# Attention with routed experts on one core: the first stacks' rows copied inside SBUF, the second batch's timetable a period later, and period 0 reordered

## The chip, the cores and the metric

The kernel runs on one core of one Trainium2 chip, and every time is a device time in microseconds (us). The core has a matrix engine, TensorE (PE, with PEld for its weight loads), VectorE (DVE), ScalarE (ACT), GpSimd (POOL) and SyncE (SP). Each runs its own instruction list in order and waits on semaphores. DMA transfers are issued here from the lists of SP and ACT, for the indirect ones from POOL.

## The reference

Input `x` has 16 batches of 512 tokens with 256 features, all float32. Two branches read a layer-normalised `x` and both are added to `x`:

```
xn = layernorm(x)
# attention, 16 heads of 16
q = rms_norm(xn @ Wq.T per head, qn_w);  k = rms_norm(xn @ Wk.T per head, kn_w);  v = xn @ Wv.T
attn = softmax(q @ k.T / 4);  A = (attn @ v) @ Wo.T
# routed experts: 8192 tokens, 8 experts, 1024 tokens each
scores = layernorm(xn) @ centroids.T
for each expert in turn: take the 1024 best tokens that are still free
F = routed + gelu(layernorm(routed) @ w1 + b1) @ w2 + b2, put back in token order
out = x + A + F
```

The products are kept close to float32 by splitting each operand into a rounded part (`hi`) and the rest (`lo`) and adding three products.

## The kernel before

**Stages.** A start-up brings in the weights and the first two batches. Then 16 batches of attention run, each in 8 periods, and in their gaps the engines prepare the next batches and route the tokens. The experts follow. The change is in the start-up and in the periods of the first batch (period 0 to 7, `at` in the code).

**One period.** `heads` (L482) makes a 128-key block of the scores of two heads; there are 32 calls per batch (`HS`) and 4 per period. Each result is turned into exponentials by ScalarE (`softmax`, L706), which needs it before PSUM's two buffers `S` come free. `weigh` (L498) multiplies them by `v`. In the same period TensorE does one item of preparation: a projection for q or k (`project_qk`, L439) or for v (`project_v`, L457), and in the first 28 periods a transposition of the normalised `x` of a later batch (`turn_x`, L415, with `score_x`, L426, for the routing scores every other period).

**From q and k to the stacks.** A projection goes from PSUM to `raw` by a DVE transposition (`turn_raw`, L839). It is squared, the squares are summed (`sum_squares`, L846), ScalarE makes the inverse root (`inverse_rms`, L685), POOL multiplies (`scale_qk`, L1216), DVE turns it back into `full` (`turn_back`, L853), and POOL splits it into `hi` and `lo` (`split_qk`, L1233). `heads` reads `stack`, in which rows 4e to 4e+3 of a tile hold hi or lo rows of one feature e for a pair of heads. Rows of 32 partitions have to be spread over every fourth partition, so `put_part` (L306) writes hi and lo to a DRAM buffer `parts`, and `stack_rows` (L321) reads them back, 6 transfers per half batch `u`. Row 3 is a constant: 0 in q's stack, 1 in k's, set by two memsets of DVE (L1047) and two of POOL (L1268).

**The first half batch.** It has its own functions, which share the squares and the scaling between ACT and POOL: `first_square`, `first_inverse_rms`, `first_round` on ACT, `first_sums`, `first_rest` on DVE and `first_scale_qk` on POOL. `first_stack` (L341) puts k's parts from SP's list (q's are put from ACT's list), and then reads the rows of the first two pairs of heads by 6 transfers (semaphore `c_stack`, 96), and of the last two by 6 more. The heads begin when `c_stack` has 96.

**The timetable.** Which period prepares what is given by `qk_at`, `v_at`, `squares_at` and `back_at` (L108 to L128), and by `scored` (L95) for the `x` of later batches. Before, the second batch (nb = 1) has its first two q and k projections ahead of period 0, together with `score_x(1)`; the other two are in periods 0 and 1, v in periods 2 and 3.

**Data for later batches.** `moments` (L768) reads an `x` tile on DVE, POOL makes the inverse deviation (`first_power`, L1185), `norm_x` (L786) normalises the tile in place in four DVE instructions, `turn_x` transposes it by TensorE. `split_x` (L1199) on POOL makes `xh` and `xl` of a batch, from which the projections read.

Of the kernel before, what the change touches and what calls it, by code (L numbers as in the profile page):

```python
# [135 lines left out]
def attention_and_routing(nc, a, out, k, ctx):  # L136
# [203 lines left out]

    def first_stack(e):  # L341

        now, then = slice(0, 2), slice(2, 4)
# [4 lines left out]
        stack_rows(e, 0, "k", 0, 0, now, c_stack)  # L350
        stack_rows(e, 0, "k", 0, 2, now, c_stack)
        e.wait_ge(s_part["k", "lo"], 16)
        stack_rows(e, 0, "k", 1, 1, now, c_stack)
        e.wait_ge(c_dve, 1)
        e.wait_ge(s_part["q", "hi"], 16)
        stack_rows(e, 0, "q", 0, 0, now, c_stack)
        stack_rows(e, 0, "q", 0, 1, now, c_stack)
        e.wait_ge(s_part["q", "lo"], 16)
        stack_rows(e, 0, "q", 1, 2, now, c_stack)
# [1483 lines left out]
```

## Time and profile before

| | us |
|---|---|
| median of 3 runs | 1056.38 (1056.06 to 1056.43) |
| the profiled execution's own time | 1055.93 |
| its span (first to last instruction) | 1054.2 |
| TensorE busy | 1023.1 (97% of the span), 6703 matmuls |
| DVE / ACT / POOL busy | 841.9 / 745.0 / 713.3 |
| start of the first `heads` call | 35.20 |

The profile counts an engine as busy while an instruction of it runs. Waits stand as idle time ahead of an instruction, with the engine that ended the wait. The granted TensorE clock is given as a share of full speed: 1.00 is 2.4 GHz and 0.50 is 1.2 GHz.

### The profile page before, as it was taken

Reading aid. Unit: us, or ns where it says so; the run is one execution under the profiler, and the core shown is the slowest. Engines: PE = TensorE matmul, PEld = TensorE weight load, DVE = VectorE, ACT = ScalarE, POOL = GpSimd, SP = SyncE. Lnnn points to the kernel's source line nnn. Section 1 sums busy time; section 2 is a strip of 40 time slices with the busy share of each in tenths; the row PEclk is TensorE's granted clock in tenths of the full one; section 3 lists DMA queues with packets and bytes.
Section 4 is the critical chain, followed back from the end, with each engine's and each line's share of the span. In section 5 each row is a group of like instructions: output and inputs, shape, how many; then the busy total and the mean of one; then the engine's idle time right before and its main releaser. Section 6 shows DMA issues by size and latency. Waiting matters only on the chain.

```text
span 1054.2 us, 19787 instructions
## 1 busy us (share of the span) xinstructions
PE 1023.1 (97%) x6703; PEld 643.0 (61%) x6703; DVE 841.9 (80%) x1922; ACT 745.0 (71%) x966; POOL 713.3 (68%) x753
## 2 busy tenths in 40 slices
PE   4899999999999999999999999999999999999997
PEld 3445555545454554454454443588888888888886
DVE  8999997787878788788778875797888788787872
ACT  3688888878888888888888889764655455465550
POOL 5677978776766767767767758666656666765434
PEclk9999999999999999999999999999999999999999
DMA  4544745344444443543533546143524344453313
GB/s 152 199 162 141 235 159 169 131 157 154 152 141 150 165 155 124 186 149 117 202 130 127 195 158 220 51 137 60 130 47 124 86 89 96 87 130 51 66 21 40
DMA packets 83527, 138.13 MB, mean 131 GB/s; under 512 B 9809, under 2 KB 35793, under 8 KB 83409
## 3 DMA queue, kind: packets, MB, share of 16 engines
q1 hardware_dynamic: 54560, 103.09, 28.7%
q0 software_dynamic: 12288, 16.79, 9.5%
q10 hardware_dynamic: 16560, 16.78, 4.9%
q8 instruction: 62, 1.02, 0.4%
q14 instruction: 57, 0.46, 0.1%
HBM read 86.28 MB, written 50.33 MB: 130 GB/s over the span
## 4 chain that ended last, share of the span: by engine, by line
PE 88%; DVE 6%; issue 2%; ACT 2%; POOL 1%; POOLq 0%; ACTq 0%; DVEq 0%
PE pv L509 19%; PE S L1476 17%; PE S L494 14%; PE W L1491 11%; PE W L453 9%; PE W L1493 6%; PE W L478 5%; PE W L464 4%; DVE xb L789 2%; ACT prob L710 1%; PE R L423 1%; PE R L1462 1%; PE pv L1462 1%; DVE raw L844 1%; PE R L434 0%
## 5 line engine op out<-in xcount | busy, mean ns | idle before, releaser
L710 ACT ACTIVATE prob<-S 128x1024 f32<-128x1024 f32 x512 | 496.1, 1023 | 91.0 <-PE S L494 90.1
L509 PE MATMUL pv<-prob,v 128*17 128x512 f32 x2048 | 246.5, 596 | 0.6 <-DVE oT L877 0.6
L494 PE MATMUL S<-stq,stk 64*128 64x512 f32 x1024 | 194.3, 452 | 5.5 <-ACT prob L710 4.1
L494 PEld LDWEIGHTS S<-stq,stk 64*128 64x128 f32 x1024 | 84.2, 184 | 130.5 <-ACT prob L710 111.7
L1758 POOL DMA_INDIRECT out<-prob,order_rows x64 | 103.4, 1615 | 58.7 <-DVE prob L1698 51.4
L509 PEld LDWEIGHTS pv<-prob,v 128*17 128x17 f32 x2048 | 46.2, 96 | 113.7 <-issue 112.3
L1554 ACT ACTIVATE wq_act<-S,b 128x512 f32<-128x512 f32 x64 | 44.0, 687 | 92.4 <-PE S L1476 92.1
L1214 POOL TENSOR_TENSOR sq<-raw 128x512 f32<-128x512 f32 x62 | 64.6, 1042 | 64.3 <-DVE raw L844 42.3
L1476 PE MATMUL S<-raw_nT,xT_w 128*128 128x512 f32 x384 | 91.2, 395 | 0.0
L1244 POOL TENSOR_TENSOR lo<-full,hi 128x512 fp32r<-128x512 f32 x62 | 80.4, 1297 | 5.0
L1476 PEld LDWEIGHTS S<-raw_nT,xT_w 128*128 128x128 f32 x384 | 71.6, 188 | 18.0 <-issue 1.7
L1476 PE MATMUL S<-hi,xT_w 128*128 128x512 f32 x256 | 81.5, 394 | 0.0
L877 DVE STREAM_TRANSPOSE oT<-pv 128x512 f32<-128x512 f32 x64 | 45.2, 707 | 31.6 <-PE pv L509 31.4
L1220 POOL TENSOR_TENSOR raw<-raw,rs 128x512 f32<-128x512 f32 x31 | 33.4, 1077 | 53.4 <-ACT rs L694 53.4
L944 DVE SCALAR_TENSOR_TENSOR ge<-R,cand 128x448 bf16<-128x448 f32 (+1 forms) x70 | 55.7, 796 | 2.6
L789 DVE TENSOR_SCALAR xb<-xb,mv,rstd 128x256 f32<-128x256 f32 x64 | 56.3, 938 | 0.8 <-POOL rstd L1190 0.8
L1554 ACT ACTIVATE wk_act<-S,b 128x512 f32<-128x512 f32 x64 | 43.9, 685 | 17.4 <-PE S L1476 16.4
L1476 PEld LDWEIGHTS S<-hi,xT_w 128*128 128x128 f32 x256 | 48.2, 188 | 11.2
L1773 POOL TENSOR_TENSOR e_va<-e_mv,eps_ln 128x4 f32<-128x4 f32 x16 | 8.3, 520 | 68.5 <-DVE e_mv L1612 68.5
L947 DVE TENSOR_REDUCE part_cnt<-ge 128x7 bf16<-128x448 bf16 (+1 forms) x70 | 51.0, 729 | 2.4
L844 DVE STREAM_TRANSPOSE raw<-W 128x512 f32<-128x512 f32 x64 | 45.0, 703 | 9.7 <-PE W L453 9.7
L453 PE MATMUL W<-xh,wq 128*128 128x512 f32 x128 | 49.8, 430 | 1.4 <-DVE xl L808 0.8
(258 smaller groups left out, 2464.1 us busy)
## 6 DMA issues: line engine op xcount, KB each, us to landing
stk<-parts SPq DMA_DIRECT2D x93, 256.0 KB, 3.8
stq<-parts SPq DMA_DIRECT2D x93, 256.0 KB, 4.3
xT<-in_w SPq DMA_DIRECT2D x32, 512.0 KB, 4.8
parts<-hi SPq DMA_DIRECT2D x63, 256.0 KB, 2.1
parts<-lo SPq DMA_DIRECT2D x63, 256.0 KB, 2.1
out<-ao ACTq DMA_DIRECT2D x32, 256.0 KB, 2.8
xb<-in_x ACTq DMA_DIRECT2D x13, 512.0 KB, 4.3
xb<-in_x SPq DMA_DIRECT2D x2, 512.0 KB, 5.7
```

Source lines behind the costliest of these rows:

```text
L453: ins = e.matmul(W[i % 2][:, :], w[n][pw][:, d, u * P:(u + 1) * P], (xh, xl)[px][nb % 2][:, d, :], start=(j == 0), stop=(j == 5))
L494: ins = e.matmul(S[n % 2][:, h, :], stack["k"][u][64 * h:64 * h + 64, p, c * P:(c + 1) * P], stack["q"][u][64 * h:64 * h + 64, p, :], star ...
L509: ins = e.matmul(pv[32 * j:32 * j + VW, :], v[b % 2][:, c, 8 * u + 4 * g + j, :], prob[(2 * t + j // 2) % RING][:, j % 2, :], start=(c == ...
L710: e.activation(prob[n % RING][:, :, :], S[n % 2][:, :, :], ACT.Exp).then_inc(s_exp, 1)
L789: ins = e.tensor_scalar(xb[m % XB][:, c, :], xb[m % XB][:, c, :], mv[m % 2][:, c, 0:1], rstd[m % 2][:, c:c + 1], ALU.subtract, ALU.mult)
L1214: e.tensor_tensor(sq[:, n, :], raw[u][:, n, :], raw[u][:, n, :], ALU.mult).then_inc(s_sq, 1)
L1244: e.tensor_tensor(lo[:, i, :], full[:, i, :], hi[:, i, :].bitcast(F32), ALU.subtract).then_inc(s_lo, 1)
L1476: ins = e.matmul(up[fc % UP], w1[pw][d][:, fc // 4, fc % 4 * P:(fc % 4 + 1) * P], nT[n % 2][px][:, d, :], start=(i == 0), stop=(i == 5))
L1491: e.matmul(down[c % 2][:, :], hid[n % 2][0][fc][:, tokens], both, start=(fc == 0), stop=(fc == NFC - 1), skip_group_check=True)
L1493: ins = e.matmul(down[c % 2][:, 0:D], hid[n % 2][1][fc][:, tokens], both[:, 0:D], start=False, stop=(fc == NFC - 1), skip_group_check=True)
L1554: e.activation(act[fc % UP], up[fc % UP], ACT.Gelu_apprx_tanh, bias=b1[:, n // U, fc:fc + 1]).then_inc(f_act, 1)
L1758: e.indirect_dma_start(out=out, out_offset=bass.IndirectOffsetOnAxis(ap=order[:, CH * n + c:CH * n + c + 1], axis=0), in_=y[u][:, c, :], i ...
```

## The change

- Rows of the first half batch's stacks, for the first two pairs of heads, are copied from `hi` and `lo` to the stack within SBUF by 12 transfers of 64 KB each (`first_rows`): 8 from SP's list (k's six, q's two of lo) and 4 from ACT's (q's rounded ones), ahead of q's `put_part`. `first_stack` keeps the way by DRAM for the last two pairs.
- q's second stack is set to zero by an ACT activation (`blank_stack`) and no longer by DVE. `tokens`, `cand` and `iota` are loaded behind `x` of batch 1 and `wo`, with a semaphore of their own (`c_table`).
- The squares of the second half of batch 0 are made by ACT (`later_square`), not POOL. DVE's order in the start-up changes: `norm_x(0)` ahead of `split_weights("q")`, `second_variance(0)` later, both `first_rest` ahead of `norm_x(1)`, and both variances and sums ahead of `split_first(1)`.
- Projections 0 and 1 of batch 1 and `score_x(1)` move from the start-up into period 0, projections 2 and 3 to periods 1 and 2, v to 3 and 4, the sums of squares to 2 and 5. With them DVE's `turn_raw(1, 0)`, both `turn_back(0, 1)`, `keep_score`, `turn_raw(1, 1)` and `moments(2)` come into period 0, and `split_weights("o")` into period 2. TensorE's wait for `wo` moves to `project_o`.
- POOL: `square(0, 3)`, `square(0, 2)` and `square(1, 0)` leave the start-up; `split_x(2)` comes in period 4, not 5.

```diff
@@ timetable
 def qk_at(nb, i):
+    if nb == 1:
+        return (0, 0, 1, 2)[i]
     return PERIODS * (nb - 2) + 6 + i if i < 2 else PERIODS * (nb - 1) + i - 2
 def v_at(nb, i):
+    if nb == 1:
+        return 3 + i
 def squares_at(nb, u):
+    if nb == 1:
+        return (2, 5)[u]
@@ attention_and_routing
-    CONSTS = 9
+    CONSTS = 6
+    TABLES = 3
+    FIRST_ROWS = 12
@@ get_stack
+        elif u:
+            e.wait_ge(c_blank, 1)
@@
+    def first_rows(e, n, part, r):
+
+        i = "qk".index(n)
+        for p in range(2):
+            e.dma_start(stack[n][0][r:P:4, p, :].bitcast(F32),
+                        (hi if part == "hi" else lo)[32 * p:32 * p + 32, i, :].bitcast(F32)).then_inc(c_stack, 16)
+
     def first_stack(e):
+        then = slice(2, 4)
+        e.wait_ge(c_pool, 1)
+        e.wait_ge(s_hi, 1)
+        first_rows(e, "k", "hi", 0)
+        first_rows(e, "k", "hi", 2)
+        e.wait_ge(s_lo, 1)
+        first_rows(e, "k", "lo", 1)
+        e.wait_ge(c_dve, 1)
+        e.wait_ge(s_lo, 2)
+        first_rows(e, "q", "lo", 2)
         put_part(e, 0, 0, "k", "hi")
         put_part(e, 0, 0, "k", "lo")
...
@@ sync_program
...
         load_x(e, 1)
         e.dma_start(land["o"], a["wo"]).then_inc(c_w["o"], 16)
+        for dst, src in ((tokens[:, :], a["tokens"]), (cand[:, :, :], a["cand"]), (iota[:, :], a["iota"])):
+            e.dma_start(dst, src).then_inc(c_table, 16)
         load_x(e, 2)
@@ project_o
+        if b == 0 and i == 0:
+            e.wait_ge(c_hi, 4)
+            e.wait_ge(c_lo, 4)
@@ heads
         if n == 0:
-            e.wait_ge(c_stack, 96)
+            e.wait_ge(c_stack, 16 * FIRST_ROWS)
+        elif n == 1:
+            e.wait_ge(s_xT, 4)
@@ tensor_program
         ins.then_inc(c_oc, 1)
-        project_qk(e, 1, 0)
-        project_qk(e, 1, 1)
-        score_x(e, 1)
-        e.wait_ge(c_hi, 4)
-        e.wait_ge(c_lo, 4)
...
                 if at:
                     weigh(e, 2 * at - 2)
+                else:
+                    project_qk(e, 1, 0)
...
-                        if m < B and qk_at(m, i) == at:
+                        if m < B and qk_at(m, i) == at and (at or i):
                             project_qk(e, m, i)
+                if at == 0:
+                    score_x(e, 1)
@@
+    def blank_stack(e):
+
+        e.wait_ge(c_zero, 1)
+        e.activation(stack["q"][1][:, :, :], zero[:, 0:1].unsqueeze(2).broadcast_to([P, 4, N]),
+                     ACT.Copy).then_inc(c_blank, 1)
+
+    def later_square(e, n):
+
+        e.wait_ge(s_raw, 4 - n)
+        e.wait_ge(c_ssq if n else s_ssq, 1)
+        e.activation(sq[:, n, :], raw[1][:, n, :], ACT.Square).then_inc(s_sq, 1)
@@ scalar_program
             e.activation(w[n][0][:, :, :], land[n], ACT.Copy).then_inc(c_hi, 1)
+        blank_stack(e)
         round_first(e, 0)
...
         first_round(e, 1)
+        later_square(e, 1)
+        later_square(e, 0)
         first_round(e, 0)
+        e.wait_ge(c_dve, 1)
+        e.wait_ge(s_hi, 2)
+        first_rows(e, "q", "hi", 0)
+        first_rows(e, "q", "hi", 1)
         put_part(e, 0, 0, "q", "hi")
         put_part(e, 0, 0, "q", "lo")
         round_first(e, 1)
+        inverse_rms(e, 0, 1)
         keep_first(e, 1)
-        inverse_rms(e, 0, 1)
@@ vector_program
-        for u in range(2):
-            ins = e.memset(stack["q"][u][:, :, :].bitcast(F32), 0.0)
-        ins.then_inc(c_dve, 1)
+        e.memset(stack["q"][0][:, :, :].bitcast(F32), 0.0).then_inc(c_dve, 1)
...
         moments(e, 0)
         split_weights(e, "k")
+        norm_x(e, 0)
         split_weights(e, "q")
-        norm_x(e, 0)
...
         first_sums(e, 1)
+        turn_raw(e, 0, 0)
         second_variance(e, 0)
-        turn_raw(e, 0, 0)
         first_sums(e, 0)
         turn_back(e, 0, 0, "k")
         turn_raw(e, 0, 3)
-        first_rest(e, 1)
         turn_raw(e, 0, 2)
         turn_back(e, 0, 0, "q")
+        first_rest(e, 1)
+        first_rest(e, 0)
         norm_x(e, 1)
-        first_rest(e, 0)
+        second_variance(e, 1)
+        sum_squares(e, 0, 1)
+        split_first(e, 1)
         copy_v(e, 0, 1)
         copy_v(e, 0, 0)
-        split_first(e, 1)
...
+                if at == 0:
+                    turn_raw(e, 1, 0)
+                    turn_back(e, 0, 1, "k")
+                    turn_back(e, 0, 1, "q")
+                    keep_score(e, 0)
+                    turn_raw(e, 1, 1)
+                    moments(e, 2)
+                    keep_score(e, 1)
...
+                if at == 2:
+                    split_weights(e, "o")
@@ split_qk (POOL)
+            if half == 1 and n == "k":
+                e.wait_ge(c_stack, 16 * FIRST_ROWS)
@@ gpsimd_program
         second_power(e, 0)
-        square(e, 0, 3)
-        square(e, 0, 2)
         second_power(e, 1)
         scale_qk(e, 0, 1)
         first_power(e, 2)
-        square(e, 1, 0)
         split_qk(e, 0, 1)
...
-                if nb < B and (back_at(nb, 0) + 1 == at):
+                if nb < B and back_at(nb, 0) + (nb > 1) == at:
                     split_qk(e, nb, 0)
...
-                if b + 2 < B and kk == (3 if b == 3 else 5):
+                if b + 2 < B and kk == {0: 4, 3: 3}.get(b, 5):
                     split_x(e, b + 2)
```

## Rows read from the trace of the kernel before

**Rows 1.** Windows: stretch, length, busy us (and instructions) per engine, clock, DMA share, GB/s.
```profile
150.00:750.00 600.00, 596.36 (x4172) 319.44 (x4173) 472.85 (x1082) 489.67 (x590) 426.26 (x454) 1.00 0.45 148
```
**Rows 2.** Timeline of PE: start, us, line, instruction, count, idle before and releaser.
```profile
27.38 1.10 PE L423 MATMUL S<-ident,xb 128*128 128x128 f32 x8 [1.35 <-DVE xb L789]
...
28.98 0.61 PE L574 MATMUL pv<-cent,onf 128*128 128x8 f32 x4
...
35.20 0.73 PE L494 MATMUL S<-stq,stk 64*128 64x512 f32 x4 [1.16 <-issue]
...
45.91 0.60 PE L423 MATMUL R<-ident,xb 128*128 128x128 f32 x4
...
47.10 1.91 PE L509 MATMUL pv<-prob,v 128*17 128x512 f32 x16
...
57.26 0.73 PE L494 MATMUL S<-stq,stk 64*128 64x512 f32 x4
```
**Rows 3.** Waits of PE from 45 to 75 us: total, times, longest.
```profile
PE R L423 <- DVE sT L828: 1.0, 1, 1.0
PE S L494 <- ACT prob L710: 0.7, 2, 0.4
PE W L453 <- POOL xl L1207: 0.5, 1, 0.5
```
**Rows 4.** Timeline of DVE, start-up and period 0.
```profile
3.43 1.76 DVE L1047 MEMSET stq<- 128x2048 f32 x1 [0.38 <-issue]
...
6.18 1.34 DVE L775 BATCH_NORM_STATS2 st<-xb 128x6 f32<-128x256 f32 x4
...
9.68 1.38 DVE L789 TENSOR_SCALAR xb<-xb,mv,rstd 128x256 f32<-128x256 f32 x4 [0.34 <-POOL rstd L1190]
...
21.22 0.70 DVE L862 STREAM_TRANSPOSE full<-raw 128x512 f32<-128x512 f32 x1
...
24.76 2.57 DVE L789 TENSOR_SCALAR xb<-xb,mv,rstd 128x256 f32<-128x256 f32 x4
27.25 0.74 DVE L821 SCALAR_TENSOR_TENSOR lo<-full,wq_col,hi 128x512 fp32r<-128x512 f32 x1
...
30.84 0.32 DVE L828 STREAM_TRANSPOSE sT<-R 128x128 f32<-128x128 f32 x1
...
31.53 1.21 DVE L851 TENSOR_REDUCE ssq<-sq 128x64 f32<-128x1024 f32 x1
...
41.31 3.83 DVE L789 TENSOR_SCALAR xb<-xb,mv,rstd 128x256 f32<-128x256 f32 x4
```
**Rows 5.** DMA issues from 0 to 60 us: queue, count, KB each, median us to landing.
```profile
xb<-in_x ACTq DMA_DIRECT2D x1, 256.0 KB, 3.9
```
**Rows 6.** Timeline of POOL.
```profile
8.30 1.34 POOL L1190 TENSOR_TENSOR rstd<-veps,half 128x4 f32<-128x4 f32 x1 [1.99 <-DVE veps L784]
...
22.00 1.06 POOL L1231 TENSOR_TENSOR raw<-raw,rs 128x512 f32<-128x512 f32 x1 [1.41 <-ACT rs L677]
```
**Rows 7.** Timeline of ACT.
```profile
12.33 0.60 ACT L659 ACTIVATE xh<-S 128x512 fp32r<-128x512 f32 x1 [4.40 <-PE S L423]
...
24.86 0.72 ACT L683 ACTIVATE hi<-full,wq_col 128x512 fp32r<-128x512 f32 x1 [2.28 <-DVE full L862]
```
**Rows 8.** Tile parts, 0 to 70 us, its DMAs from issue to landing.
```profile
DMA to landing us min/median/max: 2.0/2.8/4.3
```
**Rows 9.** Timeline of SP's DMA issues: start, us that the issuing took, count.
```profile
28.53 2.11 SPq L324 DMA_DIRECT2D stq<-parts  x3
...
46.47 1.90 SPq L324 DMA_DIRECT2D stq<-parts  x3
```
**Rows 10.** Chain that ended last, merged: start, us, engine, line, count.
```profile
38.24 2.41 PE W L453 x6
...
71.08 1.66 PE W L453 x6
```
**Rows 11.** Windows, the stretch at the lower clock; columns as in rows 1.
```profile
38.30:42.20 3.90, 3.90 (x14) 1.98 (x18) 3.00 (x6) 2.01 (x3) 3.82 (x5) 0.56 0.34 126
```

More of the change, by code:

```diff
@@ L252, in attention_and_routing @@
     c_xh = [sem(f"c_xh{m}") for m in range(2)]
-    c_x0, c_ssq, c_lg, c_rs, c_col, c_stack = (sem(f"c_{n}") for n in ("x0", "ssq", "lg", "rs", "col", "stack"))
+    c_x0, c_ssq, c_lg, c_rs, c_col, c_stack, c_table, c_zero, c_blank = (
+        sem(f"c_{n}") for n in ("x0", "ssq", "lg", "rs", "col", "stack", "table", "zero", "blank"))
     s_x = [sem(f"s_x{i}") for i in range(XB)]
@@ L339, in get_stack @@
         stack_rows(e, u, "q", 1, 2)
-    def first_stack(e):
-        now, then = slice(0, 2), slice(2, 4)
+    def first_rows(e, n, part, r):
[3 more added lines that the diff above has]
+                        (hi if part == "hi" else lo)[32 * p:32 * p + 32, i, :].bitcast(F32)).then_inc(c_stack, 16)
+    def first_stack(e):
+        then = slice(2, 4)
[8 more added lines that the diff above has]
+        first_rows(e, "q", "lo", 2)
         put_part(e, 0, 0, "k", "hi")
         put_part(e, 0, 0, "k", "lo")
-        e.wait_ge(c_pool, 1)
         e.wait_ge(s_part["k", "hi"], 16)
[L350 to L359, printed above, removed]
         stack_rows(e, 0, "k", 0, 0, then)
         stack_rows(e, 0, "k", 0, 2, then)
+        e.wait_ge(s_part["k", "lo"], 16)
         stack_rows(e, 0, "k", 1, 1, then)
+        e.wait_ge(s_part["q", "hi"], 16)
         stack_rows(e, 0, "q", 0, 0, then)
         stack_rows(e, 0, "q", 0, 1, then)
+        e.wait_ge(s_part["q", "lo"], 16)
         stack_rows(e, 0, "q", 1, 2, then)
@@ L401, in sync_program @@
                 shift_sync(e, 2 * b, 0)
-            if b:
-                put_parts(e, b, 1)
+            put_parts(e, b, 1)
             get_stack(e, b, 1)
@@ L593, in tensor_program @@
                         e.wait_ge(s_stack[u], 96 * (b + 1))
-                        e.wait_ge(c_stack, 96)
+                        e.wait_ge(c_stack, 16 * FIRST_ROWS)
+                        e.wait_ge(s_xT, 4)
                         if b or u:
@@ L1045, in vector_program @@
     def vector_program(e, x):
-        for u in range(2):
-            ins = e.memset(stack["q"][u][:, :, :].bitcast(F32), 0.0)
-        ins.then_inc(c_dve, 1)
+        e.memset(stack["q"][0][:, :, :].bitcast(F32), 0.0).then_inc(c_dve, 1)
         e.memset(pv[:, :], 0.0).then_inc(c_pv, 1)
-        for t, val in ((eps_rms, RMS_EPS), (slot, 0.0), (csum, 0.0), (zero, 0.0), (ones_h, 1.0)):
+        for t, val in ((eps_rms, RMS_EPS), (slot, 0.0), (csum, 0.0), (ones_h, 1.0)):
             e.memset(t[:, :], val)
+        e.memset(zero[:, :], 0.0).then_inc(c_zero, 1)
         e.memset(centg[:, :, :], 0.0).then_inc(c_gain, 1)
@@ L1106, in vector_program @@
                         shift_vector(e, 2 * b + kk // 4)
+                if at == 0:
[6 more added lines that the diff above has]
+                    keep_score(e, 1)
                 ex, i = routed(at)
                 if at == ROUTE:
+                    e.wait_ge(c_table, 16 * TABLES)
                     e.memset(taken, 0.0)
@@ L1128, in vector_program @@
                     for i in range(4):
-                        if m < B and qk_at(m, i) + 1 == at:
+                        if m < B and qk_at(m, i) + 1 == at and (at > 1 or m == 1 and i > 1):
                             turn_raw(e, m, i)
@@ L1239, in split_qk @@
                 e.wait_ge(s_part[n, "hi"], 16 * half)
+            if half == 1 and n == "k":
+                e.wait_ge(c_stack, 16 * FIRST_ROWS)
             e.tensor_copy(hi[:, i, :], full[:, i, :]).then_inc(s_hi, 1)
```

13 lines of the change are left out of this document (1 added, 12 removed).

## Prediction

> **What bounds the kernel now.** I read the windows first. From 150 to 750 us TensorE is busy for 596.36 of 600 us [rows 1], so in the long stretch nothing but TensorE's own work counts, and the change neither adds nor removes a matmul. It can gain only where TensorE idles: before the first heads and in the first batch. The timeline of PE gives the first: the heads begin at 35.20, after 1.16 of "issue", which no semaphore explains: it is the register load of `needed` and its branch, since TensorE's last work ended at 34.04 [rows 2]. The third view is PE's waits from 45 to 75 us: 1.0, 0.7 and 0.5, together 2.2 us [rows 3]. The fourth is the timeline of DVE, which ran through the start-up and the first periods with hardly a gap and is what TensorE waited for at 27.38 (1.35) [rows 2, 4]. After the first batch hardly a wait is left, so what TensorE is ahead at the end of batch 0 it is ahead at the end. The sum is made in the profiled execution's own terms, 1055.93 us (span 1054.2, 1.7 around it); the median of the runs is 0.45 higher, and I add that at the end.
>
> **The start of DVE.** One memset of 1.76 and the gap of 0.38 ahead of it go to ACT, 2.14 in all. The statistics of the first tile, at 6.18, need the tile's second half, which was issued at about 0.8 and took 3.9 to land: 4.7 [rows 4, 5]. Its first half can be read before that, so they begin at about 4.45 and the gain is 1.7, not 2.14. POOL does not take it back: it had idled 1.99 when it began the power at 8.30, so it is free at 6.3, and in the new order it is wanted at 6.6 [rows 6]. `norm_x(0)` moves from 9.68 to 8.0. The moved memset is an ACT activation of 2048 columns, four times the 0.60 of 512 columns: 2.4 at most, less if part of the 0.60 is fixed. ACT idled 4.40 ahead of 12.33 and must be free at 10.6, so 2.4 are hidden; without that cover it would cost itself [rows 7]. The three table loads that go behind `x` of batch 1 and `wo` free the constants sooner; `c_table` is asked for 32 periods later. Both cost nothing.
>
> **From q and k to hi and lo.** k's `full` came at 21.22, behind the sums of q's squares. It gains the 1.7, and 0.3 more because `second_variance` no longer stands ahead of `turn_raw(0, 0)`: 19.3 [rows 4]. q's scaling by POOL ended at 23.06, now 21.1, and q's turn back follows at once, at 21.2, since `first_rest` of k is moved behind it [rows 6]. ACT has two squares of 0.6 to make before it rounds q: from 20.5 to 21.8, so q's rounding starts at 21.8 in place of 24.86 [rows 7]. DVE then makes k's rest and q's rest, 0.7 each, to 23.3; q's came at 27.25 before. `norm_x(1)` follows. It took 2.57 with POOL's squares beside it and `norm_x(0)` 1.38 with POOL idle; the squares are gone, so I take 1.4, with 2.57 as the other end: done at 24.7, not 27.33 [rows 4]. TensorE turns the tile at 24.8 and has 2.2 of work to the end of the offset product (27.38 to 29.59) [rows 2]: 27.0. The two projections and `score_x(1)` that followed are now in period 0, the 1.16 stays. The heads could start at 28.2, which is 7.0 earlier.
>
> **The row transfers.** q's rounded rows are issued from ACT behind the rounding, at 22.5, four of them. The three row issues at 28.53 took 2.11 [rows 9], 0.7 each, so the last is out at 25.3; a transfer from or to `parts` landed after 2.0 to 4.3, median 2.8 [rows 8]. A copy within SBUF has no row. I take 2.4 (between the shortest and the median, since these move less): 27.7, just hidden. From 2.0 to 4.3 the rows are there from 27.3 to 29.6, so a start at 29.7 is the late end. SP's eight are issued from 20.6 on and as early. Behind ACT's four stand q's two `put_part` and `round_first(1)`, wanted at 25.4; they are done issuing near 26.0, which could delay `split_first(1)` by a few tenths. The rows of the last two pairs go out near 28 to 32 and are wanted at 41. The Trainium skill speaks against this part: "DMA: Bandwidth & Descriptors", Rules for kernel authors, says that many small transfers should be made into one and that under 64 KB one pays mostly overhead. No run here shows that yet; if it ruled, twelve transfers in place of six would eat what leaving DRAM out gives.
>
> **Period 0 and 1.** Here most of the 7.0 is lost again. After `norm_x(1)` DVE has a variance (0.5), the sum of squares (1.21), and two splits and two copies of 0.65: 29.0 [rows 4]. Projection (1, 0) waits for the last copy and takes 1.5 [rows 10]: 30.5. Then DVE's list is in series: `turn_raw` 0.65, two turns back 1.3, `keep_score` 0.7 (30.84 to 31.53), `turn_raw` 0.65: 33.8. From the statistics to the normalising it was 3.5 with a power of 1.34, the later power is 1.0: 3.2, so `norm_x(2)` starts at 37.0. POOL's `split_qk(0, 1)`, which stands behind the same power, runs beside it as it did before, when it took 3.83: 40.9 [rows 4, 6]. `turn_x(2, 0)` goes at 41.0 in place of 45.91 [rows 2]: 4.9 earlier. TensorE is there at 38.1 (period 0 ends at 33.5; then heads 1.3, weighing 1.85, a projection 1.5) and idles 2.9. At 45.91 all four projections were done; now one (1.5) is still to come: 3.4 ahead in work. The first late thing is therefore DVE, not the stack.
>
> **The rest of batch 0.** The old waits of 2.2 go, because the fuller periods 2 to 4 no longer outrun ACT, and `split_x(2)` comes a period earlier; I added up each engine's list period by period with the durations above (a normalising of four instructions lasts as long as the four POOL instructions beside it). TensorE comes to `turn_x(4, 0)` in period 5 at 61.3, and DVE is done with `norm_x(4)` and `keep_score(3)`'s transposition at 61.9, so 0.6 is left there, and 0.4 for ACT: 1.2 more. 3.4 + 1.2 = 4.6. The second half's stack: its last row issues ended at 48.4 and landed by 52.7 before period 4 began at 57.26 [rows 2, 8, 9]; now 3.1 earlier, 49.6, and wanted at 52.5. It stays hidden, with 2.9 in hand. The wait of `split_qk(0, 1)` for `c_stack` is met since 28, the new wait for `c_blank` too.
>
> **The clock.** At 38.3 to 42.2 the granted clock was 0.56 in the mean: after a stretch with few matmuls it fell to 1.2 GHz and came back [rows 11]. There a projection took 2.41 in place of 1.66 [rows 10], but TensorE would have waited for `norm_x(2)` anyway, so before it was nearly free. Now the long idle stretch is the 2.9 ahead of 41.0, and what follows is TensorE's own work. If the clock falls there for as long (3.4 us at half speed, from 0.56 over 3.9), half of it is lost: 1.7 at most; part of it may fall on waits. I take 1.6: 4.6 - 1.6 = 3.0. So the forecast is 1055.93 - 3.0 + 0.45 = 1053.4.
>
> **Rivals.**
> A, the forecast, one low stretch behind the idle time: 1053.4, its own range 1052.5 to 1054.2. Chance 0.46.
> B, no low stretch in the first periods, or one that falls on waits: 4.6 earlier, 1051.8 (to 1051.0 if `norm_x(2)` meets less of POOL). For it: idle times of 1.35 and 1.16 did not lower the clock. Against it: the new one is twice as long. Chance 0.21.
> C, the row transfers end the wait: twelve issues and landings of 4.3, or ACT's list late, start the heads at 29.7 or later and shift all behind by 1.5, and the low stretch comes too: 1054.9. Chance 0.16. This is where the Trainium skill's rule on small transfers would act.
> D, the early start is hidden anyway, no change: DVE and POOL bind the first batch so tightly that the later timetable of batch 1 (scaling, splitting and `split_x(2)` in one period and a half of POOL) gives back what period 0 gained, as a wait of 2 to 3 for `norm_x(4)` or for the projections of batch 2: 1056.2. Chance 0.11.
> E, slower: TensorE's clock stays low after the idle time of period 1 because the waits for DVE at the odd periods keep it from coming back. Each us at 1.2 GHz costs 0.5, so from 9.2 us of it on the 4.6 are gone; with 13.6 (four stretches like that of rows 11) it costs 6.8: 1055.93 + 2.2 + 0.45 = 1058.6. Against it: the one stretch of before ended by itself. Chance 0.06.
>
> **How the numbers follow.** About 0.2% (2.1 us) is what a measurement of this kernel can tell from no change, so faster means below 1054.3. A gives 0.44 of its 0.46, B 0.21, C 0.06: 0.71. Slower, above 1058.5, is only the worse part of E: 0.04. The rest, 0.25, is the same. The range leaves out the best part of B and the worse half of D and E: 1051.5 to 1056.1.
>
> **What would show it.** First statistics at 4.4 to 4.7 and `norm_x(0)` near 8.0; no DVE row for the second stack's memset; first heads at 28 to 29.7 with about 1.2 of issue ahead (right) or with a DMA ahead (C); `turn_x(2, 0)` at 41.0 with 2 to 3 us of idle time ended by DVE's `norm_x`; period 4 at 52.5; a granted clock of about 0.5 over some 3.4 us behind 41 (A) or not (B). The prediction is wrong if the heads start after 31, or if PE's waits from period 2 to 7 exceed 2 us in all.

## The result and the profile after

The changed kernel takes 1058.07 us (median of 16 runs, 1057.30 to 1059.16), the kernel before 1056.24 (16 runs, 1055.92 to 1056.94): the ratio is 1.0019, interval 1.0012 to 1.0025. That is 1.83 us slower, where 3.0 faster was forecast, and outside the range of 1051.5 to 1056.1. The profiled execution took 1057.88 with a span of 1056.1, 1.95 more than that of before.

The middle of the kernel is as it was: 596.35 us of 600 in the last line here, against 596.36 [rows 1]. The other two lines are stretches at the lower clock, and answer to [rows 11]. Windows of the changed kernel; columns as in rows 1.
```profile
29.90:33.40 3.50, 3.46 (x12) 2.21 (x10) 0.49 (x3) 1.36 (x2) 1.99 (x2) 0.53 0.70 203
43.50:47.00 3.50, 3.50 (x20) 1.30 (x23) 3.39 (x13) 2.47 (x3) 3.10 (x4) 0.53 0.74 239
150.00:750.00 600.00, 596.35 (x4177) 319.48 (x4176) 472.24 (x1083) 490.31 (x590) 426.31 (x452) 1.00 0.45 148
```
There are now two such stretches, at a mean of 0.53 of 2.4 GHz, so nearly all of each at 1.2 GHz. Before the first one TensorE had idled 1.06, 0.69 and 1.07 us with short pieces of work between; before the second it had idled 2.62. What brought the stretches on is taken up at the end. These idle times stand in the timeline of PE of the changed kernel, which answers to [rows 2]:
```profile
25.01 1.10 PE L439 MATMUL S<-ident,xb 128*128 128x128 f32 x8 [1.06 <-DVE xb L829]
...
27.92 0.50 PE L515 MATMUL S<-stq,stk 64*128 64x512 f32 x2 [0.69 <-DMA stq<-lo]
29.48 0.58 PE L515 MATMUL S<-stq,stk 64*128 64x512 f32 x2 [1.07 <-ACT xT L697]
30.11 0.77 PE L469 MATMUL W<-xh,wq 128*128 128x512 f32 x1
...
43.30 1.06 PE L439 MATMUL R<-ident,xb 128*128 128x128 f32 x4 [2.62 <-DVE xb L829]
44.29 1.22 PE L515 MATMUL S<-stq,stk 64*128 64x512 f32 x4
...
66.69 0.63 PE L439 MATMUL R<-ident,xb 128*128 128x128 f32 x4 [1.57 <-DVE sT L868]
...
73.77 1.48 PE L530 MATMUL pv<-prob,v 128*17 128x512 f32 x12 [0.61 <-DVE oT L917]
...
79.16 0.63 PE L439 MATMUL R<-ident,xb 128*128 128x128 f32 x4 [0.81 <-DVE sT L868]
```
The heads start at 27.92, 7.3 us earlier than the 35.20 of before; `turn_x(2, 0)` starts at 43.30, only 2.6 earlier. The lead is spent in period 0. What TensorE waited for from 60 us to the end (waits of PE: total, times, longest) answers to [rows 3]:
```profile
PE R L439 <- DVE sT L868: 2.9, 3, 1.6
PE S L515 <- ACT prob L743: 2.2, 7, 0.4
PE pv L530 <- DVE oT L917: 1.2, 3, 0.6
```
The timeline of DVE, which answers to [rows 4], has the start-up chain at its forecast places, then the late projection (33.05), the slow normalising (39.25), behind two small instructions of ordinary length (38.39 and 38.62), and in period 5 three small instructions that belong to the mechanism named below:
```profile
4.34 1.41 DVE L815 BATCH_NORM_STATS2 st<-xb 128x6 f32<-128x256 f32 x4 [0.21 <-DMA xb<-in_x]
...
7.90 1.38 DVE L829 TENSOR_SCALAR xb<-xb,mv,rstd 128x256 f32<-128x256 f32 x4 [0.94 <-POOL rstd L1233]
...
23.58 1.37 DVE L829 TENSOR_SCALAR xb<-xb,mv,rstd 128x256 f32<-128x256 f32 x4
...
27.48 1.29 DVE L848 TENSOR_TENSOR xl<-S,xh 128x512 fp32r<-128x512 f32 x2 [0.91 <-ACT xh L680]
28.68 1.28 DVE L908 COPY v<-W 128x512 f32<-128x512 f32 x2
...
33.05 0.72 DVE L884 STREAM_TRANSPOSE raw<-W 128x512 f32<-128x512 f32 x1 [3.01 <-PE W L469]
...
38.39 0.19 DVE L873 TENSOR_TENSOR sm<-sT,rstd 128x32 f32<-128x32 f32 x1
38.62 0.22 DVE L876 TENSOR_TENSOR scores<-sm,oc 128x32 f32<-128x32 f32 x1
39.25 4.00 DVE L829 TENSOR_SCALAR xb<-xb,mv,rstd 128x256 f32<-128x256 f32 x4 [0.41 <-POOL rstd L1233]
...
65.17 0.94 DVE L840 TENSOR_TENSOR var<-var,mv 128x4 f32<-128x4 f32 x1
...
66.58 0.92 DVE L873 TENSOR_TENSOR sm<-sT,rstd 128x32 f32<-128x32 f32 x1
67.53 1.24 DVE L876 TENSOR_TENSOR scores<-sm,oc 128x32 f32<-128x32 f32 x1
```
The timeline of ACT and of its DMA issues (ACTq), against [rows 7]: the second stack is blanked at 7.83, and from 22.16 on its list is long.
```profile
7.83 1.89 ACT L685 ACTIVATE stq<-zero 128x2048 fp32r<-128x2048 f32 x1
10.55 0.60 ACT L680 ACTIVATE xh<-S 128x512 fp32r<-128x512 f32 x1 [0.83 <-PE S L439]
...
22.16 0.72 ACT L716 ACTIVATE hi<-full,wq_col 128x512 fp32r<-128x512 f32 x1
22.96 2.70 ACTq L356 DMA_DIRECT2D stq<-hi  x4
25.71 0.60 ACTq L322 DMA_DIRECT2D parts<-hi  x1
26.35 0.45 ACTq L322 DMA_DIRECT2D parts<-lo  x1
26.85 1.09 ACT L680 ACTIVATE xh<-S 128x512 fp32r<-128x512 f32 x2 [3.97 <-PE S L439]
```
The row transfers themselves, in the DMA view from 0 to 60 us (KB each, median us to landing), beside [rows 8]:
```profile
stk<-hi SPq DMA_DIRECT2D x4, 64.0 KB, 2.1
stq<-hi ACTq DMA_DIRECT2D x4, 64.0 KB, 2.3
```
And POOL: the power for tile 2, then period 5, where `split_x(2)` of period 4 is still being worked off:
```profile
38.21 1.01 POOL L1233 TENSOR_TENSOR rstd<-veps,half 128x4 f32<-128x4 f32 x1 [6.24 <-DVE veps L824]
...
65.06 1.03 POOL L1247 CAST xh<-xT 128x1024 fp32r<-128x1024 f32 x1
66.18 2.52 POOL L1250 TENSOR_TENSOR xl<-xT,xh 128x512 fp32r<-128x512 f32 x2
```

**Where the time goes, by the starts of the periods** (first heads of each; from period 5 on both kernels have done the same matmuls, 284 at that point and 412 at period 8):

| period | 0 | 1 | 2 | 3 | 4 | 5 | 7 | 8 | 10 | 12 |
|---|---|---|---|---|---|---|---|---|---|---|
| before | 35.20 | 40.57 | 46.44 | 51.64 | 57.26 | 61.38 | 73.11 | 78.73 | 89.54 | 100.76 |
| after | 27.92 | 35.87 | 44.29 | 50.63 | 56.25 | 61.45 | 72.43 | 79.72 | 90.87 | 102.45 |

At the start of period 7 the changed kernel is still 0.68 ahead, at the start of period 8 it is 0.99 behind. Period 7 takes it 7.29 in place of 5.62, with the waits of 0.61 for `oT` and 0.81 for `sT`, both for DVE.

### The profile page after: what moved, and what is told of

Its sections match the earlier page's. It is cut to its first block, busy times and chain, and to the rows that moved or that the text cites. A ratio compares the mean times of both kernels' runs of the same rounds, so it can differ in the third digit from the quotient of the medians.

```text
span 1056.1 us, 19795 instructions
## 1 busy us (share of the span) xinstructions
PE 1024.5 (97%) x6703; PEld 643.4 (61%) x6703; DVE 839.8 (80%) x1921; ACT 747.5 (71%) x969; POOL 710.9 (67%) x751
## 4 chain that ended last, share of the span: by engine, by line
PE 87%; DVE 6%; issue 3%; POOL 2%; ACT 1%; ACTq 0%; DMA 0%; POOLq 0%; DVEq 0%
PE pv L530 19%; PE S L1518 17%; PE S L515 14%; PE W L1533 11%; PE W L469 8%; PE W L1535 6%; PE W L497 5%; PE W L480 4%; DVE xb L829 2%; ACT prob L743 1%; PE R L439 1%; PE R L1504 1%; PE pv L1504 1%; POOL rstd L1233 1%; DVE raw L884 0%
## 5 line engine op out<-in xcount | busy, mean ns | idle before, releaser
L1257 POOL TENSOR_TENSOR sq<-raw 128x512 f32<-128x512 f32 x60 | 62.4, 1041 | 64.5 <-DVE raw L884 42.5
L829 DVE TENSOR_SCALAR xb<-xb,mv,rstd 128x256 f32<-128x256 f32 x64 | 52.9, 886 | 2.2 <-POOL rstd L1233 2.2
L480 PE MATMUL W<-wv,xh 128*128 128x256 f32 x256 | 49.2, 291 | 1.3 <-DVE raw L884 1.3
```

Source lines behind the costliest of these rows:

```text
L480: ins = e.matmul(W[i][:, c * D:(c + 1) * D], (xh, xl)[px][nb % 2][:, d, at:at + P], w["v"][pw][:, d, :], start=(j == 0), stop=(j == 5))
L829: ins = e.tensor_scalar(xb[m % XB][:, c, :], xb[m % XB][:, c, :], mv[m % 2][:, c, 0:1], rstd[m % 2][:, c:c + 1], ALU.subtract, ALU.mult)
```

## The experiments

Differences are taken to the kernel before as it ran on the same chip beside each of them. Two chips gave it 1056.1 to 1056.2; on the chips of the rows from "all three" on it took 1057.5 and 1057.8, so those medians are not set against the changed kernel's 1058.07, which was measured beside 1056.24. "Both of these edits" ran on two chips and came out at -4.3 and -3.8: differences of up to 0.5 between rows of different chips tell nothing. Where the low stretches fall, and how long they last, also differs between executions of the same code: the changed kernel and the next one are the same up to period 4, and by windows of 2 us the first stretch ends near 33 in one and near 36 in the other. So the medians of 5 to 11 runs carry the verdicts, and one trace shows mechanisms only.

| kernel | median (n) | to before | ratio, interval |
|---|---|---|---|
| changed kernel | 1058.07 (16) | +1.8 | 1.0019, 1.0012 to 1.0025 |
| split_x(2) in period 5 | 1055.91 (11) | -0.3 | 0.9995, 0.9986 to 1.0004 |
| start-up alone | 1056.86 (11) | +0.7 | 1.0008, 0.9999 to 1.0017 |
| timetable alone | 1063.09 (5) | +6.9 | 1.0060, 1.0046 to 1.0074 |
| moments(2) first | 1053.62 (10) | -2.6 | 0.9974, 0.9965 to 0.9984 |
| both of these edits | 1051.81 (5) | -4.3 | 0.9959, 0.9946 to 0.9973 |
| ACT's list freed | 1056.98 (11) | +0.8 | 1.0003, 0.9994 to 1.0012 |
| spare products, late | 1056.84 (11) | +0.7 | 1.0004, 0.9995 to 1.0013 |
| spare products, both | 1055.36 (11) | -0.8 | 0.9991, 0.9982 to 1.0000 |
| all three | 1053.23 (5) | -4.3 | 0.9960, 0.9946 to 0.9974 |
| all three and spare | 1053.36 (6) | -4.1 | 0.9965, 0.9953 to 0.9977 |
| rows by way of DRAM | 1062.79 (5) | +5.3 | 1.0052, 1.0038 to 1.0066 |
| second memset on DVE | 1060.80 (5) | +3.3 | 1.0036, 1.0022 to 1.0049 |
| the three misses out | 1054.71 (8) | -3.1 | 0.9974, 0.9963 to 0.9984 |
| flag read early | 1053.06 (5) | -4.7 | 0.9958, 0.9944 to 0.9971 |
| both edits, again | 1053.99 (6) | -3.8 | 0.9966, 0.9954 to 0.9978 |

**split_x(2) back in period 5**
```diff
-                if b + 2 < B and kk == {0: 4, 3: 3}.get(b, 5):
+                if b + 2 < B and kk == (3 if b == 3 else 5):
```


> The changed kernel with one part undone: POOL's split_x(2) is back in period 5. Theory P (shared time of DVE and POOL): in the changed kernel split_x(2) ran from 65.06 to 68.7, beside DVE's small two-input instructions of period 5 (variance, keep_score), which took 0.94, 0.92 and 1.24 in place of 0.16, 0.19 and 0.22, together 2.5 us on DVE's list; undone, period 8 begins 1.3 to 2.0 earlier than in the changed kernel (79.72), and the time is 1056.0 to 1056.8. Rival K (clock): the loss is in the two stretches at 1.2 GHz near 30 and 44, which this edit does not touch: 1057.7 to 1058.2, and period 8 at 79.3 or later.

It came 2.2 below the changed kernel, and the intervals to before do not meet. Period 8 begins at 79.12, 0.6 earlier than in the changed kernel and not 1.3 to 2.0; but this execution had lost 1.2 more before period 5, by its longer low stretch. From period 5 to 8 it takes 16.50 in place of 18.27, and period 7 takes 5.63, as before the change. DVE in period 5 of this kernel:
```profile
66.36 0.16 DVE L840 TENSOR_TENSOR var<-var,mv 128x4 f32<-128x4 f32 x1
...
66.99 0.19 DVE L873 TENSOR_TENSOR sm<-sT,rstd 128x32 f32<-128x32 f32 x1
67.22 0.22 DVE L876 TENSOR_TENSOR scores<-sm,oc 128x32 f32<-128x32 f32 x1
```
The same three instructions take 0.57 together in place of 3.10, and `turn_x(4, 0)` waits 0.81 in place of 1.57. In the changed kernel each of the three ends when one of POOL's does: 65.17 + 0.94 = 66.11 (POOL's cast ends at 66.09), 66.58 + 0.92 = 67.50 (its first difference at 67.44, half of 2.52), 67.53 + 1.24 = 68.77 (68.70). So each of them began beside an element-wise instruction of POOL and ended with it. The Trainium skill has this in "SBUF — State Buffer", section "SBUF: two separate sides": of a DVE instruction with two SBUF inputs and a GpSimd instruction that reads SBUF, the one that starts first holds the shared ports for its whole length. For these three the trace agrees: 4 elements a partition took 0.94. It does not for POOL's powers of 4 columns, which read SBUF too: in the changed kernel one runs from 38.21 to 39.22, and DVE's two instructions at 38.39 and 38.62 took 0.19 and 0.22 beside it, as they did beside the power at 66.81 of this kernel. Here the page and the traces differ: it depends on which instruction of POOL is running, and why is open.

**The start-up alone** (the changed kernel with the old timetable, the old period 0 and the old place of `split_x(2)`)
```diff
-    if nb == 1:
-        return (0, 0, 1, 2)[i]
...
+        project_qk(e, 1, 0)
+        project_qk(e, 1, 1)
+        score_x(e, 1)
         e.wait_ge(c_below, 3)
```


> The start-up part alone: the changed kernel with the second batch's timetable, period 0 and split_x(2) as before the change, the inside copies of rows, blank_stack, the later squares and DVE's new start-up order kept. Theory D (DVE's list decides): the projections of batch 1 wait for DVE's copies of v, which end at 29.9 in the changed kernel, so they run at 30.0 to 33 and the heads begin at 34 to 35, no more than 1 earlier than before; time 1055.3 to 1056.3. Rival S (the start-up gain is real and the timetable eats it): heads at 32 or earlier, time 1053 to 1054.5.

Nothing is left of 7 us of earlier rows: it lies within 0.2% of before. The timeline of PE shows why (of the fastest of the 11 runs, 1055.36, the only one with a trace; its clock is 1.00 from 24 to 56 us).
```profile
30.25 0.47 PE L463 MATMUL W<-xh,wq 128*128 128x512 f32 x1 [2.88 <-DVE v L901]
...
34.59 0.73 PE L509 MATMUL S<-stq,stk 64*128 64x512 f32 x4 [0.76 <-issue]
```
The projections ahead of the heads wait 2.88 for DVE's copies of `v`, and the heads start at 34.59, only 0.6 earlier than in [rows 2]. Without a new timetable the stack was never the last thing.

**The timetable alone** (on the kernel before: `qk_at`, `v_at`, `squares_at`, period 0 and `split_x(2)` as changed, rows and memset as before)
```diff
+    if nb == 1:
+        return (0, 0, 1, 2)[i]
...
-        project_qk(e, 1, 0)
-        project_qk(e, 1, 1)
-        score_x(e, 1)
```


> The timetable alone, on the kernel before: second batch a period later, period 0 reordered, split_x(2) in period 4; rows still by DRAM, start-up order of DVE as before. The heads begin when the rows have landed, at 33 to 34, and DVE's series of period 0 (turn, two turns back, keep_score, turn, moments) follows. Theory D: it is this series that costs, so norm_x(2) starts at 42 or later and the time is 1058 to 1060, slower than both. Rival S (the timetable is neutral, the start-up part is at fault): 1055.5 to 1056.8.

It cost 6.9, the dearest kernel of all. Timeline of PE:
```profile
33.92 1.22 PE L505 MATMUL S<-stq,stk 64*128 64x512 f32 x4 [4.26 <-DMA stq<-parts]
```
TensorE idles 4.26 where the moved projections had stood, and the clock is low behind it (0.50 from 34 to 40 us). The sum of the two halves' prices alone (0.7 + 6.9) says nothing of them together (1.8): the timetable needs the earlier rows.

**moments(2) ahead of turn_raw(1, 0) in period 0**
```diff
                 if at == 0:
+                    moments(e, 2)
                     turn_raw(e, 1, 0)
...
                     turn_raw(e, 1, 1)
-                    moments(e, 2)
```


> The changed kernel with moments(2) as the first item of DVE's period 0 in place of the last but one: it falls into the 3.0 us in which DVE waited for projection (1, 0). Theory D: norm_x(2) starts near 37.0 in place of 39.25 and meets less of POOL's split_qk, turn_x(2, 0) has no wait (2.6 before) and the low clock behind it is gone (1.2 to 1.5): period 2 begins near 41, later waits for DVE take a part back; time 1055.0 to 1056.3. Rival P alone (only POOL beside DVE in period 5 counts): the same waits return in periods 5 and 7, 1057.3 to 1058.1. Rival K (clock only): 1.2 to 1.5 gained, 1056.6 to 1056.9.

It gained 4.4 on the changed kernel, more than the 1.8 to 3.1 I expected. In the changed kernel DVE idled 3.01 at 33.05 for the late projection, with the statistics of tile 2 (which need nothing of it) standing behind. Timeline of DVE here:
```profile
31.44 1.41 DVE L815 BATCH_NORM_STATS2 st<-xb 128x6 f32<-128x256 f32 x4 [1.24 <-issue]
...
38.84 1.37 DVE L829 TENSOR_SCALAR xb<-xb,mv,rstd 128x256 f32<-128x256 f32 x4
```
The power comes earlier, POOL is done with `split_qk(0, 1)` by 38.6, and `norm_x(2)` takes 1.37 in place of 4.00. TensorE goes from the projection to `turn_x(2, 0)` without a wait, and no second low stretch comes: one edit takes away the 2.62 and the low clock behind it.

**Both of these edits**

> Two edits on the changed kernel: moments(2) as DVE's first item of period 0, and split_x(2) back in period 5. Each alone gave 1053.6 and 1055.9. Theory D and P (both are load on DVE's list, at different places): in the run with moments(2) first TensorE still waited 1.6 us at turn_x(4, 0) in period 5 and 0.55 in period 11; without split_x(2) beside DVE's small instructions that falls below 0.8, and the time is 1052.2 to 1053.2. Rival (the two edits heal the same wait): 1053.4 to 1053.9.

4.3 below before. PE's wait for `sT` in period 5 is 0.8; the first wait (1.1 for `xT`) and the first low stretch are still there.

**ACT's list freed** (q's two `put_part` issued by SP)
```diff
-        put_part(e, 0, 0, "q", "hi")
-        put_part(e, 0, 0, "q", "lo")
         round_first(e, 1)
```


> The changed kernel with q's two put_part transfers issued by SP behind k's, not by ACT ahead of round_first(1). In the changed kernel ACT was busy issuing until 26.8 and DVE waited 0.91 for xh. Theory A (ACT's list delays the series that ends in norm_x(2)): projection (1, 0) at 29.2 in place of 30.1, turn_x(2, 0) 0.8 to 1.0 earlier, time 1057.0 to 1057.5. Rival (a later wait takes it): 1057.8 to 1058.2.

1.1 below the changed kernel. Projection (1, 0) starts at 29.59 in place of 30.11 and the wait for `xT` is gone, but the low stretch is not, and `turn_x(2, 0)` still waits 2.50.

**Spare products before turn_x(2, 0), then at both idle places.** These do extra work that no result uses: eight 512-column products in period 1; in the second kernel also four before the first heads and two behind their first call, ahead of the offset product.
```diff
+                if at == 1:
+                    e.wait_ge(s_sT, 2)
+                    spare(e, R[:, :], 8)
                 if scored(at - 1) is not None:
                     turn_x(e, scored(at - 1), 0)
```


> The changed kernel with eight spare 128x512 products written to R, which nothing reads, ahead of turn_x(2, 0), where TensorE idled 2.6 us. Extra work, no part of the result. Theory K (what the idle time costs is its low clock): no stretch at 1.2 GHz behind 43, period 2 takes 5.2 in place of 6.3, and the time is 1.0 to 1.5 below the changed kernel's 1058.1: 1056.6 to 1057.1. Theory D (DVE's list decides the first batch): period 2 is shorter, but the wait for keep_score(3) in period 5 grows by as much (1.6 to some 2.6), and the time stays at 1057.8 to 1058.2.

> The changed kernel with spare products at both places: eight ahead of turn_x(2, 0) as before, four in pv ahead of the first heads and two behind the first heads call, where also the offset product is moved. Extra work, no part of the result. With the clock at 2.4 GHz in period 0, projection (1, 0) takes 1.5 in place of 2.8, and DVE's series behind it starts 1.3 earlier. Theory D: this does shift the series, so norm_x(2) and all behind it come 1.0 to 1.3 earlier: 1056.6 to 1057.1. Theory K: both stretches count, 2.0 to 2.8 earlier: 1055.3 to 1056.1.

1.2 and 2.7 below the changed kernel. TensorE does more and the kernel is faster. Windows of the second kernel, over the two places:
```profile
28.00:34.00 6.00, 5.71 (x27) 3.67 (x26) 4.26 (x9) 5.01 (x9) 3.37 (x3) 1.00 0.80 267
41.00:46.00 5.00, 4.18 (x31) 1.52 (x29) 4.85 (x15) 2.43 (x3) 4.20 (x4) 1.00 0.73 260
```
The clock is 1.00 in both. So the two low stretches together were worth up to 2.7; a part of that may come from moving the offset product, which was not tried by itself.

**All three: both edits and ACT's list, then with spare products too**

> momsplit5 (1051.8) with q's two put_part transfers issued by SP as well. Theory: ACT's list held up xh, xl and the copies of v by 0.9, and nothing but TensorE's own work follows them in periods 0 to 4 of momsplit5, so most of it stays: 1050.8 to 1051.3. Rival (DVE's waits in period 5 take it): 1051.6 to 1052.0.

> allthree with the offset product moved behind the first heads call and six spare products in pv (four ahead of the first heads, two behind them; extra work, no part of the result), so that the clock does not fall to 1.2 GHz in period 0. Theory: the low stretch in momsplit5 cost 1.0 to 1.5; 0.7 to 1.3 below allthree: 1049.6 to 1050.5. Rival (DVE's waits in period 5 grow by as much): no more than 0.3 below allthree.

I expected 0.5 to 1.0 more than both edits, and 0.7 to 1.3 more again with the spare products. They came 4.3 and 4.1 below before. Both edits were 4.3 and 3.8 below it on two other chips, so a gain of up to 0.5 can't be excluded; that the gains add is not borne out. PE in the first of them:
```profile
35.46 0.65 PE L452 MATMUL R<-xT,centg 128*32 128x128 f32 x16 [1.89 <-DVE sT L868]
```
The projections are earlier, but `score_x(1)` now waits 1.89 for `keep_score(0)`, behind `moments(2)` on DVE. The idle time moved, and a low stretch with it (36.5 to 40, clock 0.54). With the spare products no low stretch is left between 24 and 50 us, but a wait of 1.4 at the same place is.

**Rows by way of DRAM, and the second memset on DVE** (each one start-up part of the changed kernel undone)
```diff
-    FIRST_ROWS = 12
+    FIRST_ROWS = 6
...
-        blank_stack(e)
         round_first(e, 0)
```


> The changed kernel with the first rows by DRAM as before the change: put_part and six transfers of 128 KB in place of twelve of 64 KB within SBUF. Theory (the inside copies are a gain): q's hi is put at 23, lands at 25 to 26, the last rows are issued by 28 and land near 30.5, so the heads begin at 30.5 to 31 in place of 27.9; projection (1, 0) stands behind the first heads call and starts at 31 to 31.5 in place of 30.1; time 1058.8 to 1060. Rival C of the prediction (many small transfers cost what leaving DRAM out gives): heads at 28.5 or earlier, 1058.1 or less.

> The changed kernel with the second memset of q's stack on DVE again. Theory: the first statistics begin 1.7 to 1.8 later (6.1), and the whole start-up with them; heads at 29.7, turn_x(2, 0) at 45.0; 1059.5 to 1060.1. Rival (the start-up is not what decides): 1058.0 to 1058.5.

They run 5.3 and 3.3 above before, so about 3.5 and 1.5 above the changed kernel by the same measure (across chips, so to 0.5): each start-up part is a gain. The first cost more than the 0.7 to 1.9 I expected, the second about what I expected (1.4 to 2.0). PE by way of DRAM:
```profile
31.08 0.96 PE L516 MATMUL S<-stq,stk 64*128 64x512 f32 x4 [3.63 <-DMA stq<-parts]
```
The heads are 3.2 later than with the direct transfers. The rule of the Trainium skill weighed before the result ("DMA: Bandwidth & Descriptors", Rules for kernel authors: make many small transfers into one, under 64 KB one pays mostly overhead) did not decide here: twelve pieces of 64 KB, landing in 2.1 to 2.3, beat the way of two steps. The rule itself was not tested. The pieces are at its bound and not under it, and no run copied the same rows inside SBUF in fewer, larger transfers.

**The three misses out, the flag read early, both edits again.** The first is the changed kernel with `split_x(2)` back, ACT's list freed and the spare products at both places. The second is both edits and DVE's load of `needed` moved:
```diff
         sum_squares(e, 0, 1)
+        e.wait_ge(c_flag, 2)
+        needed = e.value_load(flag[0:1, 0:1], min_val=0, max_val=1)
         split_first(e, 1)
```


> The changed kernel's own order of DVE, with the four things undone that the forecast left out or mis-sized: split_x(2) back in period 5, q's two put_part transfers from SP, and spare products at both places (with the offset product behind the first heads call), so that the clock stays at 2.4 GHz. Extra work, no part of the result. Theory M (the miss is the sum of these terms): alone they gave 2.2, 1.1 and 2.7 below the changed kernel's 1058.1; together 4.8 to 6.0, so 3.0 to 4.2 below the kernel before, near the 3.0 that was forecast. Rival (they heal the same wait): 1 to 2.5 below the kernel before.

> momsplit5 with DVE's load of the flag moved from the start of period 0 to ahead of split_first(1), where DVE waited 0.9 for ACT. In momsplit5 1.24 us of issue stood ahead of moments(2) at 31.96. Theory: moments(2) begins near 30.8, turn_raw(1, 0) at 33.1 in place of 33.9, and 0.4 to 0.8 of it stays: 4.7 to 5.1 below the kernel before. Rival (a load of a register stalls where it stands, for as long): the same as momsplit5, 4.1 to 4.5 below the kernel before.

> momsplit5 again, to stand beside early on the same chip: 4.1 to 4.5 below the kernel before.

With the misses out the kernel is 3.1 below before. Singly they are worth 2.2, 1.1 and 2.7, together 1.8 + 3.1 = 4.9 (across chips, so to 0.5): less than their sum of 6.0. An idle time taken away in one place that is met again in the next, as in "all three", would do that; it was not followed step by step. That 3.1 is also the forecast's figure is in part chance, for this kernel has no low stretch (forecast 1.6) and keeps PE's waits for `sT`, 1.2. Reading the flag early takes the 1.24 of issue from the place where DVE is waited for:
```profile
30.45 1.41 DVE L815 BATCH_NORM_STATS2 st<-xb 128x6 f32<-128x256 f32 x4 [0.34 <-DVE oc L1130]
...
33.09 0.72 DVE L884 STREAM_TRANSPOSE raw<-W 128x512 f32<-128x512 f32 x1 [0.62 <-PE W L469]
```
It is 0.9 below both edits on the same chip and 4.7 below before, the most of any version.

## Why the prediction was wrong, by its steps

- **The start of DVE: right.** Statistics at 4.34 (4.45 forecast), `norm_x(0)` at 7.90 (8.0), the moved memset 1.89 (2.4 at most) and hidden: 0.83 idle is left behind it.
- **From q and k to hi and lo: right.** k's `full` 19.53 (19.3), q's rounding 22.16 (21.8), `norm_x(1)` 23.58 for 1.37 (1.4), the heads at 27.92 (28.2).
- **The row transfers: right for the heads, wrong for ACT.** The heads' last wait was 0.69, for a landing, inside the bounds. It was for q's `lo` rows, which SP issued last (24.83 to 26.01), not for ACT's; and it stood where 1.16 of issue was forecast. But the issuing is work on the list of the engine that issues: four rows took 2.70 and two puts 1.05, so the list ended at 26.80 and not near 26.0, while `turn_x(1, 0)` had filled `S` by 26.11 (25.01 + 1.10). DVE idled 0.91 for that (27.48), and its last copy of `v` ended at 29.96, where 29.0 was forecast: the "few tenths" were 1.0.
- **Period 0 and 1: the first step that failed.** Projection (1, 0) was put at 29.0 for 1.5. It ran at 30.11 for 2.8: 1.1 later, most of it by ACT's list (the 0.91), and 1.3 longer by the clock. DVE's series behind it so began at 33.05, not 30.5, and `norm_x(2)` at 39.25, not 37.0. The wait for `xT`, added ahead of the second heads call, was not priced: 1.07. It held the projection back by 0.2 at most, since `v` was there at 29.96; whether it had a part in the low clock is open. The low stretch was not in the forecast at all, which read in the rows of before that idle times of 1.35 and 1.16 did not lower the clock. That reading was incomplete. The low stretch of [rows 11] stood 3 us behind the 1.16 of the kernel before, with two more idle times between, and neither is in [rows 2]:
```profile
36.82 0.49 PE L494 MATMUL S<-stq,stk 64*128 64x512 f32 x2 [0.89 <-ACT prob L710]
37.74 0.51 PE L494 MATMUL S<-stq,stk 64*128 64x512 f32 x2 [0.42 <-ACT prob L710]
```
Period 0 took 7.95 (27.92 to 35.87) where 5.3 was forecast, and `turn_x(2, 0)` came at 43.30, not 41.0. The idle time there was right (2.62 against 2.9), and so was its cause, `norm_x(2)` slowed to 4.00 by POOL (1.37 in the kernel with `moments(2)` first, where POOL is done by then).
- **The clock: its mechanism right, its number of stretches wrong.** The stretch behind the idle time came as forecast. From the start of `turn_x(2, 0)` to period 3 it is 7.33 (43.30 to 50.63) against 5.73 before (45.91 to 51.64), with the same work but for a projection for k in place of one for v, 1.5 each: it cost 1.6, the forecast's figure. The first stretch was missed. Spare products show both together at up to 2.7.
- **The rest of batch 0: wrong in sign.** `split_x(2)` a period earlier was booked inside a gain of 1.2. It costs 2.2. The lists were added up with each engine's own durations, and POOL's effect was charged on the normalising alone, not on instructions of 0.2 which, beside POOL's element-wise ones, last until those end. The trace of before held it, unread: its DVE made the same `scores` in 0.22 at 31.42, beside a power of POOL, and in 1.00 at 34.94, beside a product:
```profile
31.42 0.22 DVE L836 TENSOR_TENSOR scores<-sm,oc 128x32 f32<-128x32 f32 x1
...
34.94 1.00 DVE L836 TENSOR_TENSOR scores<-sm,oc 128x32 f32<-128x32 f32 x1
```
```profile
31.00 1.01 POOL L1197 TENSOR_TENSOR rstd<-var,half 128x4 f32<-128x4 f32 x1 [4.47 <-DVE var L802]
...
34.82 1.05 POOL L1221 TENSOR_TENSOR raw<-raw,rs 128x512 f32<-128x512 f32 x1
```
The wait at `turn_x(4, 0)` was 1.57 (0.6 forecast; 0.99 before), and in period 7 0.61 for `oT` and 0.81 for `sT` follow. The forecast's period 4 at 52.5 also left out its own 1.6 of clock; with it 54.0, and it began at 56.25.
- **Later periods: no wait was forecast.** Behind 75 us PE waits 1.4 for `sT` (0.81 and 0.55) against 0.2 before; for `oT` it is 0.6 in both. This is rival D's mechanism (the later timetable takes back what period 0 gave), with small pieces in three periods in place of one of 2 to 3.
- **Not priced, and hidden here:** DVE's load of `needed`. In the changed kernel it stands within the 3.01 in which DVE waited for the projection, so it is no part of the miss. With `moments(2)` first it comes to light, as 1.24 of issue, and moving it gave 0.9.

In the profiled executions the miss is 3.0 + 1.95 = 4.95, and the starts of the periods divide it. At period 3 the changed kernel is 1.0 ahead in time with a projection of 1.5 still to come, so 0.5 behind in work, where 3.4 - 1.6 = 1.8 ahead was forecast: 2.3, all of it `turn_x(2, 0)` at 43.30 in place of 41.0. From there to period 8 it lost another 0.5, where 1.2 more was forecast: 1.7. "split_x(2) in period 5" gives that back: 16.50 from period 5 to 8 in place of 18.27. From period 8 to the end it lost 1.0, where nothing was forecast. The three make 5.0.

Of the rivals, E had the right side and nearly the time (1058.6), by the wrong mechanism: no stretch stayed low for long, a second one came. C's time did not come (27.92, not 29.7), though its sign did, a DMA as the last wait ahead of the heads. The text's own test against itself, waits of PE over 2 us from period 2 to 7, came out against it: 1.57, 0.61 and 0.81.

What stays open is which idle times lower the clock. Here 1.06, 0.69 and 1.07 came before a fall near 29.8. In the kernel with the second memset on DVE the same three (1.06, 0.67, 1.11) were followed by a clock of 1.00 from 30 to 36, and in the start-up alone 2.88 ahead of 30.25 by 1.00 as well. So that the idle times of period 0 caused the first stretch is not shown; that filling them with products kept the clock at 1.00, in that execution, is.

## What to carry to other kernels

When work is moved in a written-out order, write down the whole list of each engine in the place where it lands, DMA issues included, and what POOL does at that moment: an instruction of 0.2 us on DVE may last until POOL's of 1 us ends. A wait in front of a series should be filled with what has no input from it (here the statistics of the next tile: 2.6 below the kernel before, 4.4 below the change as made). Such a wait can be dearer than it looks, since TensorE may come out of it at 1.2 GHz. A lead won at the start is worth only what the next engine in line can keep.

## What the runs showed of the hardware that I had not expected

- DVE's `tensor_tensor` of 4 to 32 columns: 0.16 to 0.22 alone or beside POOL's powers of 4 columns (1.01 each), 0.92 to 1.24 beside POOL's casts, products and differences of 512 columns and more, ending within 0.1 of one of them. In the kernel with `moments(2)` first the same happens at 35.51: 1.26, beside a POOL difference of 1.28 from 35.45.
- Transfers of 64 KB inside SBUF land in 2.1 to 2.3 us, but each takes 0.6 to 0.7 of the issuing engine's time; a `put_part` of 128 rows took 0.45 to 0.6 here and 0.33 to 0.36 on ACT before.
- Products that nothing uses made the kernel faster by 2.7 us (with the offset product moved), clock 1.00 in place of 0.53.
